# Expert stage of a graph network with a mixture of experts: 22-register table loads replaced by 16-register loads and six register moves

## The reference

```python
x = x + gnn(_layernorm(x), edge_index, edge_weight1, ...)      # messages, segment sum, update
tokens = _layernorm(x)
probs = softmax(tokens @ router_w.T)
rw, re = top_k(probs, 2);  rw = rw / rw.sum(-1)
out = tokens
for e in range(8):
    h = gelu(tokens @ w1[e] + b1[e])                           # w1[e], w2[e]: 256 x 256
    out = out + combine[:, e:e + 1] * (h @ w2[e] + b2[e])
return x + out
```

## Time and profile before

| | us |
|---|---|
| median of 3 runs (lowest, highest) | 3695.61 (3689.28, 3697.26) |
| the profiled execution | 3675.33 |
| its span, first to last instruction | 3673.6 |
| routing part of the expert stage and what lies before it, no PE work | to 3327 |
| expert pipeline, first PE work to last POOL scatter | 3327 to about 3599 |
| last stage | to the end |

### The profile page before, as it was taken

The page is one execution under the profiler, slowest core; times in us unless marked ns, Lnnn a source line. Parts: engine busy times, 40 slices in busy tenths (PEclk is TensorE's granted clock), DMA queues, the critical chain, the costliest instruction groups (busy, mean ns, idle before and its releaser), DMA issues. The chain is left out here.

```text
span 3673.6 us, 64517 instructions
## 1 busy us (share of the span) xinstructions
PE 2355.4 (64%) x13354; PEld 1918.8 (52%) x13355; DVE 2087.9 (57%) x6269; ACT 1607.6 (44%) x5356; POOL 2390.9 (65%) x2383
## 2 busy tenths in 40 slices
PE   0001860001888888888888888999999989107891
PEld 0001540001666666666666666787788879106781
DVE  7997860002556555656565666777777766432235
ACT  0000220001666666666666665777777756002330
POOL 0777777777888888888888875666666621483331
PEclk9999985555999999999999999999999999558995
DMA  5001330001222222222222232222222257333337
GB/s 116 2 2 12 75 63 2 2 2 30 54 51 54 52 52 52 54 51 53 52 52 52 52 52 62 64 64 63 62 65 63 63 126 207 95 84 100 106 100 223
DMA packets 175887, 237.81 MB, mean 65 GB/s; under 512 B 71575, under 2 KB 133889, under 8 KB 175323
## 3 DMA queue, kind: packets, MB, share of 16 engines
q0 software_dynamic: 85728, 144.80, 17.0%
q1 hardware_dynamic: 83082, 86.04, 8.4%
q10 hardware_dynamic: 7025, 6.40, 0.6%
HBM read 172.80 MB, written 63.30 MB: 64 GB/s over the span
## 5 line engine op out<-in xcount | busy, mean ns | idle before, releaser
L259 POOL DMA_INDIRECT edge_records<-stage x800 | 979.3, 1224 | 266.0 <-issue 212.2
L706 POOL DMA_INDIRECT work<-dst_half,stage_i x880 | 879.2, 999 | 247.3 <-issue 229.4
L936 PE MATMUL ps<-W2c,work 128*128 128x256 f32 x3520 | 872.2, 391 | 82.3 <-ACT work L874 55.4
L936 PEld LDWEIGHTS ps<-W2c,work 128*128 128x128 f32 x3520 | 642.7, 193 | 205.7 <-ACT work L874 92.4
L782 DVE TENSOR_TENSOR agg<-agg,ps 125x256 f32 x880 | 366.7, 417 | 556.4 <-remote 358.1
L945 PE MATMUL ps<-work 128*125 128x256 f32 x1760 | 469.1, 390 | 141.8 <-DVE agg L782 141.7
L861 ACT ACTIVATE work<-work 128x512 f32<-128x512 f32 x440 | 277.1, 630 | 498.4 <-DVE work L830 384.2
L945 PEld LDWEIGHTS ps<-work 128*125 128x125 f32 x1760 | 323.1, 189 | 226.9 <-issue 109.2
L855 ACT ACTIVATE work<-ps 128x256 bf16<-128x256 bf16 x440 | 164.2, 373 | 539.3 <-PE ps L906 389.0
L906 PE MATMUL ps<-identh,ebf 128*128 128x128 bf16 x880 | 124.2, 224 | 416.9 <-DVE ebf L819 380.6
L830 DVE SCALAR_TENSOR_TENSOR work<-ps,work,b2c 128x256 f32<-128x256 f32 x880 | 382.4, 476 | 10.8 <-remote 7.5
(11 more groups left out here) (206 smaller groups left out, 3209.0 us busy)
## 6 DMA issues: line engine op xcount, KB each, us to landing
work<-dst_half,stage_i POOLq DMA_INDIRECT x880
work<-routed_tokens SPq DMA_DIRECT2D x53, 257.0 KB, 2.7
routed_tokens<-rec SPq DMA_DIRECT2D x26, 514.0 KB, 4.5
edge_records<-stage POOLq DMA_INDIRECT x800
work<-expert_rows SPq DMA_DIRECT2D x25, 320.0 KB, 5.7
update_node_half<-dpart SPq DMA_DIRECT2D x50, 125.0 KB
work<-update_node_half SPq DMA_DIRECT2D x25, 250.0 KB
work<-expert_rows SPq DMA_DIRECT2D x25, 180.0 KB, 6.4
```

What stands on the lines that cost most here:

```text
L259: pool.indirect_dma_start(recd[h], bass.IndirectOffsetOnAxis(ap=stage[0:NB, i, c, 3:4].bitcast(i32), axis=0), stage[0:NB, i, c, :], None). ...
L706: pool.indirect_dma_start(bg[:, r, u, :], None, dstd, bass.IndirectOffsetOnAxis(ap=stage_i[:, c:c + 1], axis=0)).then_inc(gath[r], 16)
L936: last = t_.matmul(ps[:, 5 + s, u * D:(u + 1) * D], sT[:, a.mod(RT), u, k], W2c[:, k], start=(k == 0), stop=(k == KC - 1))
```

## The change

`enter(it)` on DVE and on PE loads only the 16 entries of the block's own eight pairs, into registers 6 to 21. The six older entries aren't read from the table again: they are moved from registers 16 to 21, where the block before left them, to registers 0 to 5. In the first block the six are set to 0.

```diff
@@ DVE, and the same on PE with t_ in place of v @@
                 def enter(it):
 
-                    v.load(regs, tabrows[0][0:1, bass.ds(it * (2 * RX) + PADT - 2 * L2, 2 * (RX + L2))])
+                    for j in range(2 * L2):
+                        v.reg_mov(regs[j], 0 if isinstance(it, int) and it == 0 else regs[2 * RX + j])
+                    v.load(regs[2 * L2:], tabrows[0][0:1, bass.ds(it * (2 * RX) + PADT, 2 * RX)])
                     offs[:] = [v.snap(r, min_val=0, max_val=(X - 1) * D) for r in regs]
```

More of the change, by code:

```diff
@@ L1541, in enter @@
                 def enter(it):
-                    t_.load(regs, tabrows[0][0:1, bass.ds(it * (2 * RX) + PADT - 2 * L2, 2 * (RX + L2))])
+                    for j in range(2 * L2):
+                        t_.reg_mov(regs[j], 0 if isinstance(it, int) and it == 0 else regs[2 * RX + j])
+                    t_.load(regs[2 * L2:], tabrows[0][0:1, bass.ds(it * (2 * RX) + PADT, 2 * RX)])
                     offs[:] = [t_.snap(r, min_val=0, max_val=(X - 1) * D) for r in regs]
```

## The result

The changed kernel takes 3660.48 us (median of 4 runs, 3659.64 to 3662.86), the kernel before 3693.83 us in the same count (3689.28 to 3697.26). The ratio is 0.9904 with a 95% interval of 0.988 to 0.9927: 33 us or 0.96% less. The forecast was 3664.5 us, 31.1 us less.

A forecast was written before the change was run, and what follows sets the result against it. PE was taken to set the expert pipeline's pace, stalled at six boundaries by table loads. 23.2 us standing still and some 8 slow clock made 31.1, DVE 0: 3695.6 - 31.1 = 3664.5 us, range 3652 to 3682.

The forecast's parts named there:

- The six boundaries: Expert pipeline, between blocks of eight pairs: cost 31.1 us, 23.2 standing still and some 8 slow clock, all saved.
- work in hand: PE at a boundary: 2.6 us of matmuls remain when the load begins; the shortened load is ready 0.5 or 0.2 us early.
- the four others lie between these: PE's other four boundaries: ready between 0.5 us early (first boundary) and 0.2 us early (second).
- Moves: PE, ahead of each load: one fused instruction of 0.18 us per block, bounds 0 and 1.1 us.
- Just in time: DVE at a boundary: ready at 3361.3 against PE's sums at 3361.56; cost 0, bounds 0 to +6 us.
- both loads have to go: Boundaries: had DVE kept its 5.29 us load, PE would wait about 2.5 us for the bank.
- same engine, same number of registers: PE's expert-stage loads: 1.11 us instead of 5.83, taken from the message stage's 16-register loads.
- the price per register: Rival on expert-stage loads: 265 ns per register, 16 take 4.24 us; 14.6 us saved, 3681 us; chance 0.04.
- The rival on the place: Something about the expert stage makes loads slow; 16 registers also take 5.8 us, nothing gained, 3696.7 us; chance 0.06.
- The Trainium skill's price: Table loads: about 200 ns per register; 16 would take 3.2 us, some 1.65 us of each stall stays, 3674 us.
- the rival with 2.75 us "without slow clock": Rival pricing loads by register: six boundary stalls of 2.75 us remain, clock not falling, 14.6 us saved; chance 0.04.
- The term of some 8 us for slow clock: PE after boundary stalls: four slow restarts, the first's eight matmuls 3.30 us instead of 1.89; some 8 us altogether.

The follow-up runs named there:

- 24 aligned: Kernel before with 24 registers loaded on both engines, from two entries earlier (word 8), the first two unused: 3672.32 us against 3700.64, ratio 0.9913.
- 22 aligned: Kernel before with its table six words lower, so the 22-register load begins at a multiple of 16 bytes: 3660.43 us against 3700.64, ratio 0.9906.
- odd table: Changed kernel with its expert-stage table one word lower (word 15, not 16): 3683.26 us against 3700.64 of the kernel before, ratio 0.9954.
- the split load: Kernel before with all 22 registers loaded by two instructions, of 16 and 6, on both engines, no moves: 3676.85 us against 3677.94, ratio 0.9998.
- The kernel with 17 registers: Changed kernel with 17 registers loaded from one word earlier and five moves, on both engines: 3665.19 us in a single run.

## Why the prediction was right, and where its reasons were not

**The time and the mechanism of the stall.** Right. The six boundaries were put at 31.1 us; the stage is 30.9 us shorter, the medians 33 us apart. The arithmetic of the work in hand (start of the load + load + 0.77 us against the moment at which the array runs dry) can be tested on loads of other durations. Lateness is read here from the starts, as what L1555 (or L1559) follows the transposes before it by, beyond the steady 0.44 us; the idle time in the lists is some 0.16 us less.

| loads at the first and second boundary, us | late by the sum | late, measured |
|---|---|---|
| 24 aligned: 1.97, 1.75 | 0.15, 0.24 | 0.15, 0.24 |
| 22 aligned: 2.18, 1.93 | 0.36, 0.42 | 0.34, 0.41 |
| odd table: 4.31, 4.20, with 0.06 for the moves | 2.55, 2.75 | 2.69, 2.88 |

That "the four others lie between these" wasn't so for the sixth boundary: with the odd table it had 2.16 us of idle time against 2.52 to 2.71 at the other five, so more work in hand. It cost nothing here.

**Moves.** Taken at 0.18 us from the nearest row, measured 0.06 us on PE and 0.075 on DVE. On PE they take from the same thin cover as the load.

**DVE.** "Just in time" at no cost, right: the only waits of PE for DVE, 0.6 us in all, are in the pipeline's first steps. That both loads have to go, with 2.5 us a boundary if DVE's stays, was right as well: 2.7.

**The step that failed is the reason for the quick load.** The text set 1.1 us for "same engine, same number of registers", and turned down the price per register because "the rows contradict a price per register in one direction or the other". They did, but the third reading was missing: both kinds of load have a price, per word where the address isn't aligned, per group of four words where it is. The rows of before held the two kinds, and the code told them apart: L774 and L896 begin at multiples of four words, L1492 and L1543 at 16 - 6 = 10. I named the entries that are loaded and not the address at which they begin. The forecast came out because the edit that leaves out six registers also moves the start from word 10 to word 16. Loading 16 registers from the old start gave nothing (the split load), and keeping 22 from an aligned one gave nearly everything. So the load's time was forecast rightly and for a wrong reason, and in this there was luck. The rival on the place was nearer to the cause than the one favoured, though not as it was put.

The Trainium skill's price (Runtime: NRT & Kernel Launch, "Instruction fetch mechanics": about 200 ns for each register, in bulk too) was said to disagree with the trace for 16 registers. For unaligned loads the trace agrees in kind, at 235 to 248 ns on DVE in the expert stage and 226 in the message stage; for aligned ones 1105 / 16 = 69 ns stands against it. The page gives its figure for register loads that the runtime adds, not for a kernel's table.

**The clock.** The text said that the clock fell after 3.85 us of standing still and not after 3.70 or 3.32, and took shorter stalls as safe (the rival with 2.75 us "without slow clock"). The kernel with 17 registers shows otherwise, in its timeline of PE:

```profile
3397.00 0.65 PE L1559 MATMUL ps<-ident,work 128*128 128x128 f32 x4 [3.00 <-issue]
3397.49 2.96 PE L1569 MATMUL ps<-ablk,work 128*128 x8
...
3436.29 1.11 PE L1559 MATMUL ps<-ident,work 128*128 128x128 f32 x4 [2.76 <-issue]
3437.19 2.85 PE L1569 MATMUL ps<-ablk,work 128*128 x8
```

And so does the odd table, at its last boundary:

```profile
3578.03 1.09 PE L1559 MATMUL ps<-ident,work 128*128 128x128 f32 x4 [2.16 <-issue]
3578.91 3.12 PE L1569 MATMUL ps<-ablk,work 128*128 x8
```

After 2.16 us the eight matmuls took 3.12 us, with a granted clock of 0.60 from 3578.9 to 3582.0 us, and after 3.70 us they took 1.89, with one of 1.00 from 3444.7 to 3448.0. With 17 registers four of six restarts were slow, behind 2.76 to 3.00 us of idle time, and those behind 2.73 and 2.40 were not. The length of one gap doesn't decide which of its two levels the clock has at the restart. The term of some 8 us for slow clock was read from rows and stays right for this kernel; as a rule about gaps it was wrong.

What stays open: why PE's loads at the six boundaries of the changed kernel vary (1107 to 1378 ns) where DVE's don't (1099 to 1107), why the first load of DVE is longer in every kernel (1845 ns in the changed one), why the slow price is lower in the message stage, what decides the clock at a restart, and how the message stage takes in slow loads.

## What to carry to other kernels

Look at what the sequencers do with tables: a load of registers isn't counted as busy and shows only as "issue" ahead of the next instruction, and it is harmless as long as it is shorter than the work that the engine has in hand. Begin such loads at a multiple of four words and load a multiple of four registers, even if that is a few more than needed (24 were quicker than 22); then count both engines that load, since the later one takes over the stall. And where one of two similar instructions is far quicker, list everything in which the two differ, the address among it, before the obvious difference is taken for the cause.

## What the runs showed of the hardware

A table load into registers (32-bit words from one partition) took, by alignment of its first word to 16 bytes (four words, counted from the start of the buffer), DVE's medians: aligned 1.10 us for 16 registers, 1.83 for 22, 1.61 for 24; not aligned 1.41 for 6, 3.93 to 3.97 for 16 (3.62 in the message stage), 4.21 for 17, 5.29 for 22. That is 0.27 us for each aligned group of four, and 0.23 to 0.25 us for each single word. For 16 registers in the expert stage it made little difference whether the start was one word below an aligned address (3.97) or two above (3.93). On PE the medians were up to 0.5 us longer.
